# MLP steps behind both sums, transform's second half with its own wait, look-up selectors from two engines: a one-core DLRM interaction kernel

## The reference

```
e = stack([tbl_f[ids[:, f]] for f in range(40)], axis=1)          # (2048, 40, 32)
z = einsum('bke,kef,bkf->bk', e[:, I], W, e[:, J])                  # 780 pairs of fields i < j
h = concat([z, dense_ctx], axis=1)                                  # (2048, 796)
h = maximum(h @ W_top1 + b_top1, 0)                                 # 512
h = maximum(h @ W_top2 + b_top2, 0)                                 # 256
y = h @ W_top3                                                      # (2048, 1)
```

## Time and profile before

| what | value |
|---|---|
| median of 3 runs | 696.76 us (696.74 to 699.01) |
| profiled execution, its own time | 699.06 us |
| its span, first to last instruction | 697.2 us |
| granted TensorE clock | 0.995 of full speed |
| TensorE busy / VectorE / ScalarE / POOL | 644.0 / 580.5 / 70.1 / 460.5 us |
| chain that ended last: TensorE / VectorE | 61% / 34% |
| first multiply | 30.9 us after the start |
| chunks 0, 1, 2, 3 begin to multiply at | 30.9, 189.2, 348.0, 510.2 us |
| last multiply ends | 661.5 us |
| MLP of the last chunk, to the end | 35.7 us |

### The profile page before, as it was taken

How to read it: one execution, slowest core, us unless ns; L and a number is a source line. 1 busy time by engine, 2 the same in 40 slices (tenths; PEclk the granted TensorE clock), 3 DMA queues, 4 the chain that set the end, 5 groups by cost and what they waited for, 6 DMA issues and landing times.

```text
span 697.2 us, 11003 instructions
## 1 busy us (share of the span) xinstructions
PE 644.0 (92%) x4800; PEld 187.3 (27%) x4800; DVE 580.5 (83%) x578; ACT 70.1 (10%) x87; POOL 460.5 (66%) x471
## 2 busy tenths in 40 slices
PE   3898988988999999999999999998999999999898
PEld 1232222222223322322222222222222222222143
DVE  6988999999978799889877889889888888888800
ACT  5502001000100100110000000100000000000002
POOL 6777777777777777777777777777777777500000
PEclk9999999999999999999999999999999999999999
DMA  8735202000000110200000200000101000000000
GB/s 322 276 98 194 69 13 74 14 13 14 13 14 15 32 58 13 74 14 13 15 13 15 76 14 14 13 14 14 16 14 15 14 14 13 12 1 1 1 0 1
DMA packets 18944, 28.28 MB, mean 41 GB/s; under 512 B 8448, under 2 KB 16016, under 8 KB 17232
## 3 DMA queue, kind: packets, MB, share of 16 engines
q0 software_dynamic: 14848, 7.63, 7.4%
q1 hardware_dynamic: 3296, 17.57, 6.5%
q10 hardware_dynamic: 752, 2.37, 0.9%
HBM read 27.53 MB, written 0.01 MB: 40 GB/s over the span
## 4 chain that ended last, share of the span: by engine, by line
PE 61%; DVE 34%; issue 3%; DMA 1%; ACT 1%; ACTq 0%; SPq 0%; DVEq 0%
DVE prods L543 26%; PE tps L567 25%; PE zps L589 15%; PE mlp_ps L636 15%; DVE hot L493 6%; PE tps L636 4%; PE mlp_ps L616 2%; DMA ids<-in_hot_ids 1%; DVE eT L500 1%; PE zps L576 1%; DVE parts L482 0%; DVE zs L482 0%; ACTq L467 0%; ACT ids L409 0%; DVE w1s L482 0%
## 5 line engine op out<-in xcount | busy, mean ns | idle before, releaser
L543 DVE TENSOR_TENSOR prods<-tps,eT 128x1024 f32<-128x1024 f32 (+1 forms) x440 | 495.1, 1168 | 72.5 <-PE tps L567 68.8
L371 POOL DMA_INDIRECT rows<-in_table,idx x464 | 459.9, 991 | 144.4 <-issue 141.2
L567 PE MATMUL tps<-eT,weights 32*128 32x512 f32 x1680 | 242.4, 641 | 33.4 <-DVE prods L543 31.1
L589 PE MATMUL zps<-prods,select 128*32 128x512 f32 x1680 | 217.7, 605 | 2.3 <-DVE prods L543 1.5
L567 PEld LDWEIGHTS tps<-eT,weights 32*128 32x128 f32 x1680 | 66.7, 183 | 185.3 <-DVE prods L543 146.4
L636 PE MATMUL mlp_ps<-zs,w1s 128*128 128x512 f32 x182 | 89.8, 615 | 0.0
L589 PEld LDWEIGHTS zps<-prods,select 128*32 128x32 f32 x1680 | 38.2, 108 | 159.4 <-DVE prods L543 98.7
L616 PE MATMUL mlp_ps<-hot,parts 128*32 128x512 bf16 x960 | 65.2, 389 | 14.7 <-DVE hot L493 10.9
L493 DVE TENSOR_SCALAR hot<-ids,code 128x2048 bf16<-128x2048 int16 (+1 forms) x88 | 67.4, 787 | 1.9 <-ACT ids L409 1.6
L387 ACT ACTIVATE zs<-zps 128x512 f32<-128x512 f32 x28 | 16.7, 598 | 326.3 <-PE zps L589 326.3
L636 PEld LDWEIGHTS mlp_ps<-zs,w1s 128*128 128x128 f32 x182 | 31.3, 189 | 55.1 <-issue 55.1
(11 more groups left out here) (31 smaller groups left out, 50.4 us busy)
## 6 DMA issues: line engine op xcount, KB each, us to landing
ids<-in_hot_ids SPq DMA_DIRECT2D x10, 1024.0 KB
rows<-in_table,idx POOLq DMA_INDIRECT x464, 2.4
zs<-in_hot_table SPq DMA_DIRECT2D x4, 512.0 KB, 7.5
w1s<-in_w ACTq DMA_DIRECT2D x1, 1792.0 KB, 7.6
weights<-in_wt SPq DMA_DIRECT2D x1, 1088.0 KB
zs<-in_hot_ids SPq DMA_DIRECT2D x1, 1024.0 KB
weights<-in_wt SPq DMA_DIRECT2D x1, 960.0 KB, 9.1
weights<-in_wt SPq DMA_DIRECT2D x1, 704.0 KB, 7.2
```

What stands on the lines that cost most here:

```text
L371: pool.indirect_dma_start(rows[:, k % ROW_SLOTS, m * EMB:(m + 1) * EMB], None, table, bass.IndirectOffsetOnAxis(ap=idx[:, g, t, m:m + 1], ...
L543: last = dve.tensor_tensor(prods[:, at % PROD_SLOTS, r:to + 1, :], tps[:, pair, r % 2:to % 2 + 1, :], eT[:, (t * GROUPS + c) % ET_SLOTS, : ...
L567: last = pe.matmul(tps[:, (2 * at + half) % PAIR_BANKS, r % 2, :], weights[part, n, :], eT[part, slot, :], start=True, stop=True)
L589: last = pe.matmul(zps[EMB * r:EMB * (r + 1), :], select[:, off:off + EMB], prods[:, at % PROD_SLOTS, r, :], start=kt < KT - 1 and n == fi ...
```

## The change

- **Cycles.** A chunk's first quad is a cycle by itself, and then come pairs (1, 2), (3, 4), ..., in every chunk. A cycle is now T(at), R(at-1), first half of the MLP steps, look-ups, T(at+1), R(at), second half of the steps, look-ups: a block of two steps becomes one and one, a block of three two and one.
- **Wait of the transform.** Half 0 waits for `multiplied >= 2*at - 2`, half 1 for `2*at - 1`.
- **Look-ups.** `HOT_COUNT = (4, 4, 2, 2)`: group (1, 3) is looked up too, as the first of chunk 1, since its table's parts lie in `w1s`. 12 groups are looked up, 28 gathered. Chunk 0 makes and looks up 32 units for chunk 1 instead of 24.
- **ScalarE makes units**: 5 of 8 in chunk 1's groups and 4 of 8 in those of chunks 2 and 3, 36 in all, each with two ACTIVATEs over 128 x 2048: Abs of (id minus code), then Relu of (1 minus that), the second waiting on the first. VectorE makes the other 52 (88 before).
- **Made ahead** by 4 quads everywhere (before: 2 in chunk 0). The shortening of group 4's ids moves from the cycle of quad 4 to that of quad 3; the five DMAs that load the MLP's weights move from behind group 3's look-up to behind group 4's (quad 16), on ScalarE's queue.
- **MLP of chunk 2** goes in blocks into consecutive cycles of chunk 3 (before: spread out), and six of the 28 first-layer steps of chunk 3's own MLP (column tile 0, k 0 to 5) run in chunk 3, one each at n = 37, 39, 41, 43, 45, 51.
- `eT` has 14 slots instead of 13.

```diff
-ROW_SLOTS, ET_SLOTS, PROD_SLOTS = 6, 13, 3
+ROW_SLOTS, ET_SLOTS, PROD_SLOTS = 6, 14, 3
-HOT_COUNT = (4, 3, 2, 2)
-HOTS = [(t, g) for t in range(CHUNKS) for g in range(HOT_COUNT[t])]
+HOT_COUNT = (4, 4, 2, 2)
+HOTS = [(t, g) for t in range(CHUNKS) for g in ((3, 0, 1, 2) if t == 1 else range(HOT_COUNT[t]))]
...
+CYCLES = [at for t in range(CHUNKS) for at in [(t * QUADS,)] + [(t * QUADS + n, t * QUADS + n + 1) for n in range(1, QUADS, 2)]]
...
-        for k, block in enumerate(blocks):
-            at = cycles[k if hots else k * len(cycles) // len(blocks)]
+        for at, block in zip(twos, blocks):
...
+    for k, n in enumerate(EARLY_AT):
+        sides[(CHUNKS - 1) * QUADS + n].append(("mlp", CHUNKS - 1, 0, 0, k))
...
+EARLY_AT = (37, 39, 41, 43, 45, 51)
...
+def by_scalar(h, u):
+    return HOTS[h][0] == 1 and u not in (1, 4, 7) or HOTS[h][0] > 1 and u % 2 == 1
...
-MADE_AHEAD = (2, 4, 4, 4)
+MADE_AHEAD = 4
...
-            MAKES[side_at - MADE_AHEAD[side_at // QUADS]].append(item[1:])
+            MAKES[max(side_at - MADE_AHEAD, min(side_at, 4))].append(item[1:])
...
-SHORTENED_AT = {max(at // 2 * 2 - 4, 4): h for h, at in FIRST_MADE.items() if h >= HOT_COUNT[0]}
+SHORTENED_AT = {max(at - (at % QUADS + 1) % 2 - 4, 3): h for h, at in FIRST_MADE.items() if h >= HOT_COUNT[0]}
...
+            def make_unit(h, u):
+                if u == [by_scalar(h, u_) for u_ in range(UNITS)].index(True):
+                    act.wait_ge(ids_short, h + 1)
+                act.wait_ge(hot_used, h * UNITS + u - HOT_SLOTS + 1)
+                columns = hot[:, (h * UNITS + u) % HOT_SLOTS].rearrange("p q c -> p (q c)")
+                act.activation(columns, ids16[:, h % 2].rearrange("p q c -> p (q c)"), ACT.Abs,
+                               bias=minus_code[:, u:u + 1]).then_inc(distances, 1)
+                act.wait_ge(distances, made_until(h, u, True))
+                act.activation(columns, columns, ACT.Relu, scale=-1.0, bias=ones[:, 0:1]).then_inc(hot_made_act, 1)
...
             def transform(at):
-                wait(pe, multiplied, 2 * at - 1)
                 for half in range(2):
+                    wait(pe, multiplied, 2 * at + half - PAIR_BANKS + 1)
...
-            for at in range(0, TOTAL, 2):
-                steps, between = steps_of(at)
-                if at == QUADS // 2 * 2:
+            for cycle in CYCLES:
+                at = cycle[0]
+                steps = steps_of(at)
+                if at == QUADS:
                     pe.wait_ge(mlp_loaded, 16 * 5)
+                halfway = (len(steps) + 1) // 2
                 transform(at)
-                for _, t, layer, m, k in steps[:len(steps) - between]:
+                if at > 0:
+                    reduce(at - 1)
+                for _, t, layer, m, k in steps[:halfway]:
                     mlp(t, between_banks, layer, m, k)
-                if not steps and at > 0:
-                    reduce(at - 1)
                 look_ups(at)
-                transform(at + 1)
-                if steps:
-                    reduce(at - 1)
-                for _, t, layer, m, k in steps[len(steps) - between:]:
-                    mlp(t, between_banks, layer, m, k)
-                reduce(at)
-                look_ups(at + 1)
+                if len(cycle) == 2:
+                    transform(at + 1)
+                    reduce(at)
+                    for _, t, layer, m, k in steps[halfway:]:
+                        mlp(t, between_banks, layer, m, k)
+                    look_ups(at + 1)
...
-                        mlp(CHUNKS - 1, last_banks, layer, m, k)
+                        if ("mlp", CHUNKS - 1, layer, m, k) not in EARLY:
+                            mlp(CHUNKS - 1, last_banks, layer, m, k)
```

More of the change, by code:

```diff
@@ L143, in plan_sides @@
         hots = [h for h, (t_, _) in enumerate(HOTS) if t_ == t + 1]
-        cycles = [at for at in range(0, TOTAL, 2) if t * QUADS <= at < (t + 1) * QUADS]
+        twos = [cycle[0] for cycle in CYCLES if len(cycle) == 2 and cycle[0] // QUADS == t]
         first = 3 * M1
@@ L156, in plan_sides, with made_until @@
                 sides[at] += block
+    for k, n in enumerate(EARLY_AT):
+        sides[(CHUNKS - 1) * QUADS + n].append(("mlp", CHUNKS - 1, 0, 0, k))
     return sides
+EARLY_AT = (37, 39, 41, 43, 45, 51)
 SIDES = plan_sides()
[L163 removed]
+EARLY = [("mlp", CHUNKS - 1, 0, 0, k) for k in range(len(EARLY_AT))]
+def by_scalar(h, u):
+    return HOTS[h][0] == 1 and u not in (1, 4, 7) or HOTS[h][0] > 1 and u % 2 == 1
+def made_until(h, u, scalar):
+    return sum(by_scalar(h_, u_) == scalar for h_ in range(len(HOTS)) for u_ in range(UNITS) if (h_, u_) <= (h, u))
+MADE_AHEAD = 4
 MAKES = {at: [] for at in range(TOTAL)}
@@ L170 @@
         if item[0] == "hot" and item[1] >= HOT_COUNT[0]:
-            MAKES[side_at - MADE_AHEAD[side_at // QUADS]].append(item[1:])
+            MAKES[max(side_at - MADE_AHEAD, min(side_at, 4))].append(item[1:])
 def steps_of(at):
-    steps = [item for item in SIDES[at] if item[0] == "mlp"]
-    return steps, int(len(steps) > 0 and at % QUADS % PER_KT == 0)
+    return [item for item in SIDES[at] if item[0] == "mlp"]
 def use_of(item):
@@ L189 @@
 FIRST_MADE = {unit[0]: at for at, made in MAKES.items() for unit in made if unit[1] == 0}
-SHORTENED_AT = {max(at // 2 * 2 - 4, 4): h for h, at in FIRST_MADE.items() if h >= HOT_COUNT[0]}
-assert len(SHORTENED_AT) == len(HOTS) - HOT_COUNT[0]
+SHORTENED_AT = {max(at - (at % QUADS + 1) % 2 - 4, 3): h for h, at in FIRST_MADE.items() if h >= HOT_COUNT[0]}
+assert len(SHORTENED_AT) == len(HOTS) - HOT_COUNT[0] and set(SHORTENED_AT) <= {cycle[0] for cycle in CYCLES}
 def wait(engine, semaphore, count):
@@ L199, in hots_until @@
 def hots_until(t, g):
-    return sum(h <= (t, g) for h in HOTS)
+    return HOTS.index((t, g)) + 1
 def gathered_until(t, g):
@@ L274, in build @@
         remainder = sem("remainder")
-        hot_made = sem("hot_made")
+        hot_made_dve = sem("hot_made_dve")
+        hot_made_act = sem("hot_made_act")
+        codes_turned = sem("codes_turned")
+        distances = sem("distances")
         hot_used = sem("hot_used")
@@ L447, in _ @@
             round_part(3, 1)
+            act.wait_ge(code_built, 1)
+            act.activation(minus_code[:, :], code[:, :], ACT.Copy, scale=-1.0).then_inc(codes_turned, 1)
+            act.wait_ge(codes_turned, 1)
+            act.wait_ge(consts_built, 2 + Q)
             shorten(3)
-            for at in range(0, TOTAL, 2):
+            for cycle in CYCLES:
+                at = cycle[0]
                 if at in SHORTENED_AT:
                     shorten(SHORTENED_AT[at])
-                if at == QUADS // 2 * 2:
+                if at == QUADS:
                     act.wait_ge(mlp_loaded, 16 * 5)
-                steps, between = steps_of(at)
-                if not between:
-                    drain_tiles(steps)
+                drain_tiles(steps_of(at))
                 drain_sums(at - 1)
[L458 to L461, removed]
+                if len(cycle) == 2:
+                    drain_sums(at)
+                for kind, *step in [item for quad in cycle for item in SIDES[quad]]:
                     if kind == "hot" and step[1] == UNITS - 1:
                         drain_hot(step[0])
-                        if step[0] == HOT_COUNT[0] - 1:
+                        if HOTS[step[0]] == (1, HOT_GROUPS - 1):
                             for dst, src in ((w1s, w1), (w2s, w2), (w3s, w3), (b1s, b1), (b2s, b2)):
                                 act.dma_start(dst[:], src).then_inc(mlp_loaded, 16)
+                for unit in [unit for quad in cycle for unit in MAKES[quad]]:
+                    if by_scalar(*unit):
+                        make_unit(*unit)
             drain_z(CHUNKS - 1, KT - 1)
@@ L489, in make_unit @@
                     dve.wait_ge(code_built, 1)
-                elif u == (2 if h == 0 else 0):
+                elif u == (2 if h == 0 else [by_scalar(h, u_) for u_ in range(UNITS)].index(False)):
                     dve.wait_ge(ids_short, h + 1)
@@ L549, in _ @@
                 for unit in MAKES[at]:
-                    make_unit(*unit)
+                    if not by_scalar(*unit):
+                        make_unit(*unit)
                 if at == 0:
```

22 lines of the change are left out of this document (15 added, 7 removed).

## The result

The changed kernel takes 696.67 us (median of 20 runs, 696.35 to 697.92), the kernel before 698.66 in the runs beside it (20 runs, 696.74 to 700.43). The ratio is 0.9978, 95% interval 0.997 to 0.9986: about 1.5 us faster, where 5.7 were forecast. In a second set of runs it is 0.9988 (0.9976 to 1.0001), so a gain of 1.5 us is at the edge of what can be told. The profiled execution has a span of 696.1 us, the one before 697.2.

What follows compares the result with a forecast made beforehand. VectorE was taken as the nearer bound in chunk 0, TensorE in chunks 1, 2 and the tail, with gaps in both in chunk 3. Terms -4 - 2 + 2.1 - 1.4 + 4.7 - 5.1 = -5.7 gave 691.1 us, range 685 to 697.

Steps and rivals of the forecast that it cites:

- The block prices: TensorE's distances to the next block in MLP cycles: transform 1.07 us, sum before a step 1.00, step 1.06; two-step cycle 6.26.
- the head: First multiply to quad 6: waits for group 4's shortened ids go, -2 us (0 to -4).
- A unit on ScalarE: Two ACTIVATEs of 1.99 us each, about 4.1 with the wait between; expected in time in chunk 0, at cost 0.
- The plain quad: Quads without steps or look-ups: earlier half 0 brings the 2.45 us ring down to VectorE's 2.27, or 2.3.
- the signs named for being wrong: Two-step cycles taking 5.9 us, or TensorE waiting for ScalarE for more than 3 us in chunk 0.
- 5 x 5.19: Chunk 3: five cycles with an early step, each at 5.19 us, within the sum by cycles.
- the 156.7 of the cycles: Chunk 3's length in us summed by cycles, taken as 156, which is +4.7.
- the second term that was mis-sized: Chunk 0, quads 6 to 52: 127 us, -4, with bounds 118.6 and 130.9.
- VectorE's sum: Chunk 0, quads 6 to 52: VectorE's work falls from 126.1 to 118.2 us, as it makes 12 units.
- TensorE's sum of 118.6: Chunk 0, quads 6 to 52: TensorE's work in us, eight more look-ups adding 5.4.
- the first rival: Chunk 0's gain doesn't come: it stays at 130.9, chunks 1 and 2 lose another 1; 696 us, chance 20%.
- the order's term: MLP steps behind both sums: 0.34 us more a cycle in chunks 1 to 3, about 16 us.

Runs made afterwards that it cites:

- E2: The changed kernel without the six early MLP steps in chunk 3, put back in the tail: 696.09 us, ratio 0.9981.
- E5: E1 with 24 look-ups in chunk 0 instead of 32 (11 looked-up groups, 29 gathered): 674.93 us, ratio 0.9674 against the kernel before.
- E8: E5 without the six early MLP steps in chunk 3: 677.12 us, ratio 0.97 against the kernel before.
- B2: The kernel before with only the transform's wait split by halves: 691.85 us, ratio 0.9916.
- E4: The changed kernel with all units made on VectorE, none on ScalarE: 707.97 us, ratio 1.016 against the kernel before.
- B3: The kernel before with only group 4's ids shortened two quads earlier: 696.21 us, ratio 0.9973.
- E1: The changed kernel with all MLP steps of a cycle again between its two transforms, both sums behind: 677.68 us, ratio 0.9722 against the kernel before.
- B1: The kernel before with only the new order of the MLP cycles: 709.89 us, ratio 1.0174.

## Why the prediction was wrong

*What held.* The time fell, but by 1.5 us where 5.7 were forecast. The block prices and the term they gave were right: +2.0 and -1.4 in chunks 1 and 2, forecast +2.1 and -1.4; two-step cycles at 6.25; quads 1 to 24 of chunk 1 at 78.68, forecast 78.6; the tail -5.1; the head -2.0 at full clock, forecast -2. A unit on ScalarE is 1.995 + 2.002 us, forecast 4.1 with the wait. It comes in time: in chunk 0 TensorE waits 0.6 us for ScalarE's units and 2.9 for its copies, the look-up at quad 40 among them. The plain quad fell from 2.45 to 2.29 (4.58 for two), forecast 2.27 to 2.3. None of the signs named for being wrong came: they watched the two-step cycle and ScalarE, and the miss lay elsewhere.

*The step that failed: "5 x 5.19", chunk 3.* The prediction took an early step's cycle for TensorE's sum of blocks, which leaves out the wait for the product. Quads 37 to 46 took 28.23 us, not 25.95, and the two cycles behind them (dense inputs; n = 51) 5.57 and 5.79 instead of 5.2 and 5.1; the 156.7 of the cycles had been rounded to 156 on top. Chunk 3 took 159.80 us, +8.55 and not +4.7: 3.8 us missing. What the runs showed in its place: between plain quads neither engine bounds, the ring does, and what stands between a sum and the next transform is paid nearly in full (E2: 0.96 a step, E5 and E8: 0.54 when it stands between the transforms).

*Chunk 0 is the second term that was mis-sized:* at full clock it gave 2.0 and not 4. VectorE's sum held (119.61 busy, forecast 118.2). TensorE's sum of 118.6 cannot be read from its busy time (127.21 of 128.61), as a block that stands waiting counts as busy (1.51 us for the transform at 631.19, against 1.14). The loss above 118.6 was 10 us where the forecast took 8.4. The look-up at quad 40, 1.4 later than its price, was not foreseen, and the eight look-ups more cost 2.5 (E5). Chunks 3 and 0 together miss 5.8 us, which is the whole forecast gain.

*Luck.* The profiled execution that the forecast started from was 2.3 us above the median. The prediction corrected the total for it, but read the head and chunk 0 as they stood, at a clock of 0.91 in the head. That the medians still show 1.5 us, and in the direction forecast, comes from the clock. The time of 696.67 is also the 696 of the first rival, but not by its mechanism: chunk 0 did come down, and chunks 1 and 2 lost nothing more.

*Where the gain went.* Measured apart: the split wait -5.9 (B2; -7 at equal clock), ScalarE's units about -12 (E4), shortening earlier -1 to -2 (B3), early steps 0 (E2), the twelfth group about +3 (E1 to E5); and the order of the MLP blocks **+19** (E1; +12 alone on the kernel before, B1). The parts overlap and don't add up exactly, but no other part comes near the order's +19. The fourteenth slot of `eT`, units made 4 quads ahead in chunk 0 and the placing of chunk 2's MLP in consecutive cycles were not measured apart. The prediction had the order's term, 16 us, and the ones against it; it did not say plainly that all the rest of the change was worth about as much. The section on the change says that VectorE makes 52 units; it makes 60 (96 less ScalarE's 36, and 60 in the trace).

*The rule of the Trainium skill on changing the tiling mode* (TensorEngine Tiling (Array Packing), Tiling Modes) agrees with the rows: sum to look-up 0.89, sum to step 0.99, with 0.86 of matmuls in the sum in either case. What in the change of shape takes the time, no run separates. The rule of the Trainium skill on relu (ScalarE: Activation LUTs, Rules for kernel authors) is right on the price, 4.0 against 0.66, and following it would have cost about 12 us in this kernel (E4), as ScalarE was busy for only 70.1 us before.

## What to carry to other kernels

Count the changes of matmul shape in a loop, not only the matmuls: where TensorE is full, T R M T R M took 0.34 us more than T M T R R with its 5.9 a cycle, which is 16 of the 19 us in the whole. Where no engine is full, find the ring (here multiply, sum, transform, multiply) and ask of each added block whether it stands in it; the sum of the engine's blocks is only a lower bound there. Test the parts of a combined change one by one: here three of them were gains, hidden by one that cost as much. Before two traces are compared stretch by stretch, compare their granted clock: here two short dips to 0.50 put 2.3 us into the head.

## What was not expected

- Splitting one wait by halves, though the four matmuls run at once and end together, gained 5.9 us alone: where it has to wait, the second pair of matmuls then runs behind the first (1.51 to 1.61 us from such a transform to the next block, instead of 1.07), and a plain quad takes 2.29 instead of 2.45, close to VectorE's own 2.27.
- In the first 24 quads of chunk 1 TensorE is 78.55 of 78.68 us busy (75.10 of 75.10 before): a fuller timeline for the same work. The busy share can't tell the 0.34 us of shape changes from work; the distance between blocks can.
- In 38 of 43 executions of the kernel before the mean clock was below 1.000, with a median of 697.17 us at 0.998 and 698.86 at 0.995 against 696.43 at 1.000; in the changed kernel it was at 0.999 or more in 29 of 30. What in the two heads decides it, no run here shows.
